# A decoder layer on one core: hidden-layer matmuls on square tiles, in two turns with the coefficient matmuls between

## What is computed

```python
q = (xn @ w_q.T).reshape(b, s, 2, NH, KD).transpose(2, 0, 1, 3, 4)   # xn: x, normalised over all tokens
sim = jnp.einsum('pbnhd,hkpd->pbnhk', q, keys_p)
scores, idx = jax.lax.top_k(sim, K)                       # K = 8, NH = 8, 64 keys
all_scores = (scores[0][..., :, None] + scores[1][..., None, :]).reshape(b, s, NH, K * K)
sc, pk = jax.lax.top_k(all_scores, K)
indices = jnp.take_along_axis(all_idx, pk, axis=-1)       # all_idx = idx0 * 64 + idx1
hmid = jnp.einsum('bnd,bnhkd->bnhk', inputs, down[indices])
hmid = jax.nn.sigmoid(sc) * jax.nn.gelu(hmid, approximate=False)
return jnp.einsum('bnhk,bnhkd->bnd', hmid, up[indices])
```

## Time and profile before

| | us |
|---|---|
| median of 3 runs | 3022.41 (3021.91 to 3024.26) |
| profiled execution | 3019.98, of it span 3018.2 |
| granted TensorE clock, mean | 0.945 |
| PE busy | 2683.1 (89%) |
| DVE busy | 2232.2 (74%) |
| ACT, POOL busy | 741.0 (25%), 796.6 (26%) |
| H matmuls (L1015), busy | 952.3 |
| output matmuls (L1044), busy | 911.3 |
| A matmuls (L1030), busy | 307.2 |
| score matmuls (L991), busy | 242.6 |

### The profile page before, as it was taken

How to read it: one execution, slowest core, us unless ns; L and a number is a source line. 1 busy time by engine, 2 the same in 40 slices (tenths; PEclk the granted TensorE clock), 3 DMA queues, 4 the chain that set the end, 5 groups by cost and what they waited for, 6 DMA issues and landing times.

```text
span 3018.2 us, 104697 instructions
## 1 busy us (share of the span) xinstructions
PE 2683.1 (89%) x43108; PEld 2287.9 (76%) x43108; DVE 2232.2 (74%) x7540; ACT 741.0 (25%) x1302; POOL 796.6 (26%) x604
## 2 busy tenths in 40 slices
PE   7961037779999999999999999999999999999996
PEld 5841025658888888888888888888888888888895
DVE  5657867377777777777777777777777777777754
ACT  4730025312222222222222222222222222222210
POOL 1330000033333333333333333333333333333332
PEclk9985569889999999999999999999999999999997
DMA  5550025900000000000000000000000000000000
GB/s 174 174 169 0 0 60 161 180 2 13 13 13 13 13 13 13 13 13 13 13 13 13 13 13 13 13 13 13 13 13 13 13 13 13 13 13 13 9 10 12
DMA packets 84638, 99.51 MB, mean 33 GB/s; under 512 B 6189, under 2 KB 74702, under 8 KB 84046
## 3 DMA queue, kind: packets, MB, share of 16 engines
q1 hardware_dynamic: 84190, 92.94, 10.9%
HBM read 65.13 MB, written 27.79 MB: 31 GB/s over the span
## 4 chain that ended last, share of the span: by engine, by line
PE 79%; issue 1%; DVE 1%; DMA 0%; SPq 0%; ACT 0%; DVEq 0%; POOL 0%; ACTq 0%; POOLq 0%
PE bank L1015 31%; PE bank L1044 30%; PE bank L1030 9%; PE bank L991 8%; PE bank L980 1%; DVE hot L1221 1%; PE bank L1003 1%; DMA gelh<-in_table 0%; SPq L940 0%; DVE gelh L1233 0%; DVE top_i L1177 0%; POOL hot L962 0%; DVE top L1173 0%; ACT dnT L1137 0%; DVEq L1242 0%
## 5 line engine op out<-in xcount | busy, mean ns | idle before, releaser
L962 POOL TENSOR_TENSOR hot<-hot,valsT 128x512 f32<-128x512 f32 x512 | 732.9, 1450 | 2039.6 <-DVE hot L1221 2039.6
L1015 PE MATMUL bank<-x2T,dnT 128*64 128x128 f32 x16384 | 952.3, 275 | 3.6 <-issue 3.2
L1015 PEld LDWEIGHTS bank<-x2T,dnT 128*64 128x64 f32 x16384 | 891.7, 137 | 27.7 <-issue 15.0
L1044 PE MATMUL bank<-up,gelh 64*128 64x256 f32 x8192 | 911.3, 379 | 1.5 <-DVE gelh L1233 1.5
L1044 PEld LDWEIGHTS bank<-up,gelh 64*128 64x128 f32 x8192 | 786.6, 187 | 140.3 <-issue 50.8
L1221 DVE TENSOR_TENSOR hot<-iota,valsT 128x1024 f32<-128x1024 f32 x512 | 652.5, 1315 | 30.8 <-ACT valsT L1120 30.8
L1233 DVE TENSOR_TENSOR gelh<-bank,gelh 128x512 f32<-128x512 f32 x512 | 329.8, 686 | 230.7 <-PE bank L1030 230.1
L1125 ACT ACTIVATE gelh<-bank 128x512 f32<-128x512 f32 x512 | 299.1, 597 | 684.2 <-PE bank L1015 683.6
L1030 PE MATMUL bank<-hot 64*64 64x64 f32 x16384 | 307.2, 224 | 41.3 <-issue 23.7
L1030 PEld LDWEIGHTS bank<-hot 64*64 64x64 f32 x16384 | 270.2, 137 | 92.3 <-issue 92.3
L1173 DVE MAX8 top<-bank 128x8 f32<-128x64 f32 x1024 | 140.9, 217 | 260.9 <-PE bank L991 252.7
(11 more groups left out here) (143 smaller groups left out, 1868.8 us busy)
## 6 DMA issues: line engine op xcount, KB each, us to landing
x_scratch<-x_sb SPq DMA_DIRECT2D x64, 256.0 KB, 2.2
xT_sb<-in_xT SPq DMA_DIRECT2D x32, 256.0 KB, 2.9
x_sb<-in_x SPq DMA_DIRECT2D x32, 256.0 KB, 2.9
x_again<-x_scratch SPq DMA_DIRECT2D x32, 256.0 KB, 2.7
x_tile<-x_scratch SPq DMA_DIRECT2D x32, 256.0 KB, 3.7
up<-in_table SPq DMA_DIRECT2D x2, 4096.0 KB, 42.1
yo<-x_scratch SPq DMA_DIRECT2D x32, 256.0 KB, 2.8
out_y<-yo SPq DMA_DIRECT2D x32, 256.0 KB, 2.0
```

What stands on the lines that cost most here:

```text
L962: pool.tensor_tensor(lo, lo, valsT[:, par, 2, TQ * q:TQ * (q + 1), None].to_broadcast([P, TQ, NK]), ALU.mult).then_inc(gated_ready, 1)
L1015: mm = pe.matmul(ps_h[q % 2][half(c), i, :], dnT[:, k, lo // 2, half(lo % 2)], x2T[:, k, c, :], start=(k == 0), stop=(k == CC - 1))
L1044: mm = pe.matmul(ps_out[c], gelh[half(c), par, lo, :], up[half(c), lo, :], start=(lo == 0), stop=(lo == NK - 1))
```

## The change

- `hidden` is called per n and turn. A product with 128 weight rows becomes two with 64 rows: on 64x64 tiles, four of which make up the array. In turn 0 the upper half of the rows goes to one bank of a pair and the lower half to the other, in turn 1 the other way round, accumulating. Bank pairs are (3, 4) and (0, 1) by the parity of n. Turn 1 waits for `half_mm`, which counts turns 0.
- PE's step is H turn 0, A, H turn 1 for each n; `turn_vals(g+1)` and `turn(g+2)` both stand after A at n=5; both scores follow n=7, then the output in one piece.
- `gelu` does two banks per call; ACT converts the new tile at n=5 into an x2T of two buffers. x2_tile has one buffer.
- Scores use banks (3, 4) and (0, 1), for group 1 banks (5, 6) and (2, 7); the transposed tile uses bank 7.
- The opening: turn and both scores of groups 0 and 1 first, then the down table's transposes over two banks, then H(0) with `turn_vals(0)` inside; the load of tile 1 stands behind the down table's on SP; on DVE `route(1, 0)` comes ahead of the first one-hots.

The core of the diff:

```diff
-            ps_score = bank[0], bank[1]
-            ps_xT = bank[0][:, :].rearrange("p (k n) -> p k n", k=CC)
+            ps_score = (bank[3], bank[4]), (bank[0], bank[1])
+            ps_score1 = (bank[5], bank[6]), (bank[2], bank[7])
+            ps_xT = bank[7][:, :].rearrange("p (k n) -> p k n", k=CC)
...
-            ps_h = [bank[3 + i][:, :].rearrange("p (l m) -> p l m", l=LQ) for i in range(2)]
+            ps_vals0 = bank[5][:, 0:3 * P].rearrange("p (v t) -> p v t", v=3)
+            ps_h = [[bank[i][:, :].rearrange("p (l m) -> p l m", l=LQ) for i in two] for two in ((3, 4), (0, 1))]
...
-            ps_dn = [bank[3 + i][:, :].rearrange("p (k c e) -> p k c e", k=CC, c=2) for i in range(4)]
+            ps_dn = [bank[3 + i][:, :].rearrange("p (k c e) -> p k c e", k=CC, c=2) for i in range(2)]
...
-                def load_tile(g, par):
-                    sp.wait_ge(xT_mm, g - 1)
-                    sp.dma_start(x2_tile[:, par], one(x2g, g)).then_inc(x2_in[par], 16)
+                def load_tile(g):
+                    sp.wait_ge(xT_mm, g)
+                    sp.dma_start(x2_tile[:, :, :], one(x2g, g)).then_inc(x2_in, 16)
...
                         sp.dma_start(dn[half(b), some, :], by_parity[b][:, some, 0:C]).then_inc(dn_in[i], 16)
+                load_tile(1)
...
                     if later(g, 1):
-                        pe.wait_ge(scores_read, 2 * g)
                         pe.wait_ge(x2T_ready, g)
                         pe.wait_ge(xn_ready, g)
+                    if isinstance(g, int) and g == 2:
+                        pe.wait_ge(scores_read, 4)
+                    if later(g, 3):
+                        pe.wait_ge(sum3_done, g - 2)
...
-                    if later(g, 1) or a:
-                        pe.wait_ge(scores_read, 2 * g + a)
+                    if later(g, 2):
+                        pe.wait_ge(gel_ready, g * NA - 1 + a)
...
+                    if isinstance(g, int) and g < 2:
+                        pe.wait_ge(scores_read, 3 + g)
...
-                def hidden(g, q):
-                    pe.wait_ge(x2T_ready, g + 1)
-                    if later(g, 1) or q >= 2:
-                        pe.wait_ge(gel_ready, g * NQ + (q - 1))
+                def hidden(g, par, n, turn):
+                    if turn == 0:
+                        pe.wait_ge(x2T_ready, g + 1)
+                        if n < 2:
+                            pe.wait_ge(scores_read, 2 * g + (n + 1))
+                            if later(g, 1):
+                                pe.wait_ge(gel_ready, g * NA - 1 + n)
+                        else:
+                            pe.wait_ge(gel_ready, g * NA + (n - 1))
+                    else:
+                        pe.wait_ge(half_mm, g * NA + (n + 1))
+                    rest(pe, pe_rests)
                     for i in range(LQ):
-                        lo = LQ * q + i
                         for k in range(CC):
-                            for c in range(2):
-                                mm = pe.matmul(ps_h[q % 2][half(c), i, :], dnT[:, k, lo // 2, half(lo % 2)], x2T[:, k, c, :],
-                                               start=(k == 0), stop=(k == CC - 1))
-                    mm.then_inc(h_mm, 1)
+                            for h in range(2):
+                                s = h if turn == 0 else 1 - h
+                                lo = 2 * LQ * n + LQ * s + i
+                                for c in range(2):
+                                    mm = pe.matmul(ps_h[n % 2][s][half(c), i, :], dnT[half(h), k, lo // 2, half(lo % 2)],
+                                                   x2T[half(h), par, k, c, :], start=(turn == 0 and i == 0 and k == 0),
+                                                   stop=(turn == 1 and i == LQ - 1 and k == CC - 1),
+                                                   skip_group_check=True)
+                    mm.then_inc(h_mm if turn == 1 else half_mm, 1)
...
-                def output(g, par, some):
-                    if some[0] == 0:
-                        pe.wait_ge(coef_ready, NA * (g + 1))
-                        if within(g, 1):
-                            pe.wait_ge(valsT_ready, g + 2)
-                        if later(g, 1):
-                            pe.wait_ge(sum3_done, g)
-                    for lo in some:
+                def output(g, par):
+                    pe.wait_ge(coef_ready, NA * (g + 1))
+                    if within(g, 1):
+                        pe.wait_ge(valsT_ready, g + 2)
+                    if within(g, 2):
+                        pe.wait_ge(x2T_ready, g + 3)
+                        pe.wait_ge(xn_ready, g + 3)
+                    if later(g, 1):
+                        pe.wait_ge(sum3_done, g)
+                    for lo in range(NK):
                         for c in range(2):
                             mm = pe.matmul(ps_out[c], gelh[half(c), par, lo, :], up[half(c), lo, :],
                                            start=(lo == 0), stop=(lo == NK - 1))
-                    if some[-1] == NK - 1:
-                        mm.then_inc(out_mm, 1)
-                turn(0, 0)
+                    mm.then_inc(out_mm, 1)
+                turn(0)
                 score(0, 0)
+                score(0, 1)
+                turn(1)
+                score(1, 0)
+                score(1, 1)
+                pe.wait_ge(scores_read, 1)
                 for q in range(NQ):
                     if q % 4 == 0:
                         pe.wait_ge(dn_in[q // 4], 32)
-                    if q >= 4:
-                        pe.wait_ge(dnT_ready, q - 3)
+                    if q >= 2:
+                        pe.wait_ge(dnT_ready, q - 1)
                     for k in range(CC):
                         for c in range(2):
-                            mm = pe.transpose(ps_dn[q % 4][:, k, c, :], dn[:, 2 * q + c, k * P:(k + 1) * P], ident[:, :])
+                            mm = pe.transpose(ps_dn[q % 2][:, k, c, :], dn[:, 2 * q + c, k * P:(k + 1) * P], ident[:, :])
                     mm.then_inc(dnT_mm, 1)
                 pe.wait_ge(dnT_ready, NQ)
-                score(0, 1)
-                for q in range(NQ):
-                    hidden(0, q)
-                turn(1, 1)
-                score(1, 0)
-                turn_vals(0)
-                score(1, 1)
+                for n in range(0, NA, 2):
+                    hidden(0, 0, n, 0)
+                    hidden(0, 0, n + 1, 0)
+                    hidden(0, 0, n, 1)
+                    hidden(0, 0, n + 1, 1)
+                    if n == 2:
+                        turn_vals(0)
                 pe.wait_ge(up_in, 32)
                 def step(g, par):
                     for n in range(NA):
+                        if within(g, 1):
+                            hidden(g + 1, 1 - par, n, 0)
                         coefs(g, n)
                         if n == 5 and within(g, 1):
                             turn_vals(g + 1)
-                        if n == NA - 1 and within(g, 2):
-                            turn(g + 2, par)
+                            if within(g, 2):
+                                turn(g + 2)
                         if within(g, 1):
-                            hidden(g + 1, 2 * n)
-                            hidden(g + 1, 2 * n + 1)
-                    output(g, par, range(0, 8))
+                            hidden(g + 1, 1 - par, n, 1)
                     if within(g, 2):
                         score(g + 2, 0)
-                    output(g, par, range(8, 24))
-                    if within(g, 2):
                         score(g + 2, 1)
-                    output(g, par, range(24, NK))
+                    output(g, par)
                 groups(pe, step)
...
-                def raw_in(g):
-                    if later(g, 1):
-                        act.wait_ge(h_mm, NQ * g)
+                def raw_in(g, par):
+                    if later(g, 2):
+                        act.wait_ge(h_mm, NA * (g - 1))
                     rest(act, act_rests)
-                    act.activation(x2T[:, :, :, :].rearrange("p k c m -> p k m c"),
+                    act.activation(x2T[:, par].rearrange("p k c m -> p k m c"),
                                    ps_xT.rearrange("p k (m c) -> p k m c", c=2), ACT.Copy).then_inc(x2T_ready, 1)
...
-                def gelu(g, par, q):
-                    act.wait_ge(h_mm, g * NQ + (q + 1))
+                    act.activation(valsT[:, par], vals_of(g), ACT.Copy).then_inc(valsT_ready, 1)
+                def gelu(g, par, n):
+                    act.wait_ge(h_mm, g * NA + (n + 1))
                     rest(act, act_rests)
-                    act.activation(gelh[:, par, LQ * q:LQ * (q + 1), :], ps_h[q % 2], ACT.Gelu).then_inc(gel_ready, 1)
+                    for s in range(2):
+                        at = 2 * LQ * n + LQ * s
+                        last = act.activation(gelh[:, par, at:at + LQ, :], ps_h[n % 2][s], ACT.Gelu)
```

(82 more changed lines are left out.)

12 lines of the change are left out of this document (5 added, 7 removed).

## The result

The changed kernel takes 3236.58 us (median of 4 runs, 3232.32 to 3240.19) where the kernel before took 3022.16 beside it: a ratio of 1.0708, 95% interval 1.0689 to 1.0726. It is 214 us slower; forecast were 172 more, 3194 us, in a range that ends at 3270. The profiled execution took 3232.32 us with a span of 3230.6.

What follows compares the result with a forecast made beforehand. PE, busy 89%, was taken to bound the kernel and to starve for instruction packets after the change. Steps 1 to 29 +172.6 us, step 30 +7, step 0 with opening -7.5: +172, 3194 us; range 3040 to 3270.

Steps and rivals of the forecast that it cites:

- The bound and the direction: PE bounds every step; with more instructions in H and A it is starved of packets, so slower, chance 0.82.
- Rival (a): The shape-change drain is saved and PE isn't starved: steps save 2.7 us, 2925 us in all, chance 0.15.
- Rival (b): PE starved, but with a shorter packet cycle of 3.1 to 3.5 us: steps 73 to 77 us, 2965 to 3080, chance 0.06.
- Rival (c): Square H tiles don't overlap four at a time: H doubles, +28 us a step, about 3890 us, chance 0.02.
- Step and cycle: Starved H and A on PE take a 256-instruction packet per 3.83 us: 45.9 us, step 80.8, 5.95 more.
- about 1.5 are in hand: At the start of H and A, after the slow output, about 1.5 packets go at 3.0 us each, 4.5 us.
- The change of shape: On PE, 18 fewer runs of one tile shape per step save 0.15 us each, 2.7 us, leaving 71.7 unstarved.
- A between the turns: The wait for H's first turn costs nothing behind A of 1.09 us; bare, it would expose some 0.2 us.
- Scores, transposes, output's new wait: Gathered scores and transposes, and output() waiting for ACT's conversions of bank 7, cost nothing; cover gone, 2.1 us.
- Just covered: DVE and GpSimd chain: A(2) comes 8.77 us after A(0); an unstarved n takes 4.45 us, A(2) after 8.9.
- Well covered: DVE and GpSimd chain when PE is starved: each n takes 5.7 us, so PE shouldn't wait for it.
- Opening: H(0) from 577 to about 616, first H of step 0 at 617.5; gain 13.5 us, between 5 and 20.

## Why the prediction was right, point by point

**The bound and the direction.** PE's stream was the path; the chain of after and the old kernel with split columns (3250 us) show that the number of instructions alone makes the loss. Rival (a) fails in this kernel, and its number for the step (71.7) stands for a kernel with the old number of instructions. The Trainium skill, "Runtime: NRT & Kernel Launch", section Instruction fetch mechanics, gives PE a buffer of 128 KiB: no run bears that out, since eight packets in hand would have carried two thirds of an A/H part, and the changed kernel pauses behind 32 records. The same section's two 16 KiB lines fit better: no step of after ran more than 2.8 packets before its first pause. Rival (b) fails: its cycle of 3.1 to 3.5 us is below that of every step. Rival (c) fails too: four tiles at once took 3.46 to 3.50 us per n.

**Step and cycle.** Predicted 3.83 us a packet. From the end of the first pause to that of the last, a packet takes 3.77 us in the step shown first and 3.97 in the next (35.87 us for 9.03 packets); over steps 2 to 29 it is 3.67 to 4.06, on average 3.87, alike in both kinds of step, and a landing is 1.42 us ahead of the use (1.37 predicted). Output and scores: 34.9 predicted, 34.96 measured. The A/H part: 45.9 predicted; 47.44 in the step shown and 47.33 in the next (1682.13 to the scores at 1729.46), on average 48.0 at the loop's top and 46.4 in the steps between; a step is 82.02 on average instead of 80.8. So the cycle was right, and the term that was too small is the start of the part, "about 1.5 are in hand" at full pace. At the loop's top there are 64 instructions and then a pause: nearly all 12.3 packets cost a cycle, 12.3 x 3.83 = 47.1. In the other steps more was in hand than the prediction said (2.8 packets before the first pause, mostly), which by its sum gives 2.8 x 3.0 + 9.5 x 3.83 = 44.8; but the first pause, mostly 0.8 to 1.4 us, comes on top and had no term. In 29 steps the difference (7.14 against 5.95) makes 35 of the 40 us that the sum fell short.

**The change of shape.** 0.15 us a run predicted, 0.16 to 0.19 in the rows of A and H with 256 columns, 0.15 in those of output, scores and transposes, and 71.71 for the step's sum. Right.

**A between the turns.** Right that it costs nothing with A there; "bare some 0.2 us" was too little: 0.40 per n, and 4.7 us a step with what follows from it.

**Scores, transposes, output's new wait.** Nothing predicted, and no wait for ACT or DVE stands in the chain of the steps shown.

**DVE and POOL.** "Just covered" holds: 8.66 us when it is bare, 9.0 in the kernel with 256 columns (1624.51 to 1633.52). "Well covered" when starved is not quite so: in three of the steps of after A(7) waits for POOL, 0.28 us (`1151.88 1.16 PE bank L1060 x64`).

**Opening.** The chain of after (L1161 gelu, the rest as in the step above):

```profile
536.41 12.45 DMA x_tile<-x_scratch
...
574.48 3.72 PE bank L1040 x126
578.20 5.29 issue
583.48 6.74 PE bank L1040 x127
590.22 0.95 issue
...
602.50 5.18 DVE hot L1263 x3
...
616.73 1.28 ACT L1161
...
619.37 2.84 PE bank L1040 x64
```

Tile 1 landed at 548.9 (550.5 with the wait), H(0) began at 574.5 (577), the first H of step 0 at 619.4 (617.5). H(0) ended at 616.0, as predicted (616), and not before 605. A packet under the table load took 9.0 and 7.7 us (3.72 + 5.29, 6.74 + 0.95), not 9.4 each time; but what ended last was the order on DVE and ACT, the last route behind the first one-hots, then gates and gelu, which the prediction had named. Step 1 began 4.3 us earlier instead of 7.5, as step 0 took 83.45 us and not 82.0. The last steps: +9.6 against +7.

**The range.** It was set by the cycle (3.5 to 4.05 us) and held the result; single steps had 3.67 to 4.06. A bound for the packets in hand, from none to two, was missing beside it; with none the A/H part comes to 12.3 x 3.83 = 47.1 us, near the 47.2 that it took on average. That the range of the cycle also covered this term was luck.

## What to carry to other kernels

On an engine that is the bound, count instructions as well as array time: over an A/H part PE got 256 instructions every 3.87 us and no faster, and splitting matmuls to save array time lost 10.4 us a step (82.1 against 71.7) where it saved 3.2. A slow stretch ahead saved up at most 2.8 packets, counted to the first pause, and next to nothing across the loop's jump; one short fast stretch between slow ones was free, as with square tiles for the last n of eight. When a piece is moved ahead of a producer's trigger (A(0) here), look at the chain that starts there, even if its engine is only 75% busy.

## What was not expected of the hardware

Two half-size matmuls in place of one cost little by themselves (3.88 us against 3.65 per H) until the packets limit them. A wait between two runs of dependent matmuls costs 0.40 us where 0.14 us of "issue" is all that the chain names; most of the rest is a slower start of the run behind it (1.96 against 1.76 us), and later packets on top. And instruction packets come later beside a data load: under the table load q8's packets start 8.1 us apart in after (580.67 to 588.81) and 9.2 to 9.4 in the old kernel with split columns, more than twice the 3.87 of the quiet steps, though each travels only 1.1 to 1.4 us there, against 0.9 to 1.6 elsewhere. The delay lies before the transfer.
